# Reversing TensorE's three jobs of a step in the maximum rounds of a four-stage graph network

## The reference

```
for l in range(3):
    xi, xj = x[dst], x[src]
    m = concatenate([xi, xj - xi], axis=-1)
    h = relu(m @ W1[l] + b1[l])
    h = h @ W2[l] + b2[l]
    x = relu(segment_max(h, dst))
x = layernorm(x_before + x)
```

## Time and profile before

| | |
|---|---|
| two executions, median | 8951.76 us (8947.82 to 8955.71) |
| span of the profiled execution, first to last instruction | 8953.9 us |
| the profiled execution's own time | within the two above as far as its span tells; the page gives the span alone |
| TensorE matmul busy | 6143.5 us, 69% of the span |
| TensorE weight load busy | 3185.8 us, 36% |
| GpSimd busy | 5682.7 us, 63% |
| VectorE busy | 4170.1 us, 47% |
| ScalarE busy | 2476.2 us, 28% |
| TensorE on the chain that ended last | 41% of the span |

### The profile page before, as it was taken

The page is one execution under the profiler, slowest core; times in us unless marked ns, Lnnn a source line. Parts: engine busy times, 40 slices in busy tenths (PEclk is TensorE's granted clock), DMA queues, the critical chain, the costliest instruction groups (busy, mean ns, idle before and its releaser), DMA issues.

```text
span 8953.9 us, 145246 instructions
## 1 busy us (share of the span) xinstructions
PE 6143.5 (69%) x26339; PEld 3185.8 (36%) x26339; DVE 4170.1 (47%) x5692; ACT 2476.2 (28%) x6097; POOL 5682.7 (63%) x5873
## 2 busy tenths in 40 slices
PE   1333336666656666666333359999899999899997
PEld 0111124444434444443222224444344444344443
DVE  4444449999958999971333322222222222222222
ACT  0111114444434444431111112222222222222222
POOL 4777756666636666642777756666566666566665
PEclk9999996666656666655555555555555555555555
DMA  4666646666636565642333334444444444444443
GB/s 105 171 169 169 171 114 132 130 131 130 130 84 132 130 130 129 130 98 75 66 66 66 66 72 103 102 102 102 90 99 102 103 102 102 87 103 103 102 103 85
DMA packets 1847481, 981.41 MB, mean 110 GB/s; under 512 B 1290750, under 2 KB 1685374, under 8 KB 1847422
## 3 DMA queue, kind: packets, MB, share of 16 engines
q1 hardware_dynamic: 1660030, 786.84, 35.9%
q0 software_dynamic: 187392, 193.93, 13.3%
HBM read 714.25 MB, written 265.65 MB: 109 GB/s over the span
## 4 chain that ended last, share of the span: by engine, by line
PE 41%; issue 6%; POOL 6%; DVE 1%; ACT 1%; DMA 0%; SPq 0%; POOLq 0%; DVEq 0%
PE ps L847 13%; PE ps L824 12%; PE ps L820 10%; POOL rows L707 5%; PE ps L854 4%; PE ps L452 1%; PE ps L503 1%; PE ps L445 0%; POOL agg L717 0%; DMA rows<-src_table,idx 0%; DMA agg<-states_sum,last_i 0%; DVE split_r L326 0%; ACT split L317 0%; DVE split L328 0%; DMA states_sum<-hb 0%
## 5 line engine op out<-in xcount | busy, mean ns | idle before, releaser
L707 POOL DMA_INDIRECT rows<-src_table,idx x5656 | 5480.8, 969 | 2954.7 <-issue 1541.6
L820 PE MATMUL ps<-ident,rows 128*64 128x128 f32 x5656 | 1807.6, 405 | 1527.1 <-issue 738.9
L925 DVE TENSOR_TENSOR_SCAN st<-pen,st,ps 64x512 f32<-64x512 f32 x603 | 766.9, 1272 | 2696.9 <-PE ps L847 2692.1
L820 PEld LDWEIGHTS ps<-ident,rows 128*64 128x64 f32 x5656 | 773.1, 145 | 2038.4 <-issue 1766.2
L854 PEld LDWEIGHTS ps<-ident,st 64*128 64x128 f32 (+1 forms) x5656 | 797.7, 212 | 1584.9 <-issue 1555.0
L824 PE MATMUL ps<-sel,win 128*64 128x128 fp8e4 x7272 | 1281.9, 314 | 0.0
L847 PE MATMUL ps<-xe,w 64*64 64x512 f32 x1212 | 1190.1, 1083 | 0.0
L833 PE MATMUL ps<-sel,win 128*97 128x128 fp8e4 x4848 | 516.0, 282 | 837.4 <-issue 821.3
L754 ACT ACTIVATE pen<-sel 64x512 f32<-64x512 fp8e4 (+1 forms) x1010 | 628.1, 622 | 1468.3 <-DVE decay L989 1468.3
L854 PE MATMUL ps<-ident,st 64*128 64x64 f32 (+1 forms) x5656 | 1010.4, 330 | 23.5 <-DVE st L925 23.5
L759 ACT ACTIVATE hb<-ps 128x256 f32<-128x256 f32 (+1 forms) x1414 | 578.9, 409 | 1519.5 <-PE ps L854 819.4
(11 more groups left out here) (133 smaller groups left out, 3352.5 us busy)
## 6 DMA issues: line engine op xcount, KB each, us to landing
states_sum<-hb SPq DMA_DIRECT2D x1010, 128.0 KB
sel<-onehots SPq DMA_DIRECT2D x1010, 128.0 KB
win<-dst_table SPq DMA_DIRECT2D x1616, 72.8 KB
win<-dst_table SPq DMA_DIRECT2D x2424, 48.0 KB
rows<-src_table,idx POOLq DMA_INDIRECT x5656, 2.5
states_att<-hb SPq DMA_DIRECT2D x404, 194.0 KB
dst_b<-in_dst_row SPq DMA_DIRECT2D x202, 256.0 KB, 3.7
prev_b<-in_dst_prev SPq DMA_DIRECT2D x202, 256.0 KB, 4.4
```

Of the source, the lines that this page charges most:

```text
L707: pool.indirect_dma_start(rows[:, s, j, :], None, srcs[q.r], bass.IndirectOffsetOnAxis(ap=idx[:, s, j:j + 1], axis=0))\
L820: last = nc.tensor.matmul(o, rows[:, s, j, :], ident[:, :], is_transpose=True, start=True, stop=k != MAX)
L925: nc.vector.tensor_tensor_scan(st[0:kw, s % V, :], d0, d1, init, op0, op1).then_inc(q.st_ready.sem, 1)
```

## The change

In the MAX rounds the order of TensorE's list is reversed. The lags stay: in step t TensorE now transposes chunk t-2 back, lifts chunk t-1, and then turns chunk t. Nothing else differs; the instructions, their operands, waits and semaphores are the same, and so are all other engines' streams.

```
                 if k == ATT:
                     chunks(pe, (0, turn), (0, query), (1, score), (3, back))
                 elif k == MAX:
-                    chunks(pe, (0, turn), (1, lift), (2, back))
+                    chunks(pe, (2, back), (1, lift), (0, turn))
                 else:
                     chunks(pe, (0, turn), (1, back))
                 node_pe(pe, q)
```

## The result

The changed kernel took 9125.08 us (two executions, 9124.70 and 9125.46) against 8951.76 us: 173 us more, a ratio of 1.0194 with a 95% interval of 1.0175 to 1.0214. It is slower clear of the noise. The ratio itself is just inside 2%, but the interval has that line inside it.

A forecast was written before the change was run, and what follows sets the result against it. TensorE's full queue was taken to bound the MAX rounds; 3 rounds x (198 steps x 0.31 us + 0.9) = 187 us more, giving 9139 us, 2.1% slower; its own range 9109 to 9210, for 8 in 10 9098 to 9215.

The forecast's parts named there:

- TensorE's queue bounds the MAX rounds: MAX rounds: TensorE busy 1000 us of 1000, a step of 5.76 us, so each microsecond it stands still lengthens the program.
- The lift's stall: Lift behind its relu: starts 0.15 after turning, takes 0.68, plus latency, less back's 0.62; 0.31 us a step, 0.26 to 0.43.
- x: Latency from the relu's end until TensorE starts the lift: estimated 0.10 us, between 0.05 (node phase) and 0.22 (REL loop).
- The side of the 2% line: Relu exposed, 9109 to 9210 us, chance 0.81: 0.50 above the 2% line at 9131 us, 0.31 below.
- The weight load: Lift's weights: by the skill's rule the load could slip under back, up to 0.14 off each step, sum 104 us; given little.
- Back, penalty and scan at no cost: MAX step: scan over 1.62 us into the 3.25 of turning, 1.6 us of cover left; penalty doesn't hold up the scan.
- The ends of a round: First chunks of a MAX round 2.5 us longer, the end after the last turning 1.6 shorter: net 0.9 us a round.
- The sign to look for: Trace after: idle before the lift (L847), put down to ScalarE's xe (L777), about 0.3 us in some 600 steps.
- Rival C: TensorE's instruction stream refilled after each stall, or ScalarE late to the relu: 0.53 us a step, 9270 us; chance 0.07.
- Rival B: Back or an early load covers more of the relu: stall below 0.2 us, 8955 to 9056 us; chance 0.07.
- Rival D: Clock rises in the MAX rounds, at the joint of lift and turning: up to 460 us less, 8490 us; chance 0.05.
- The earlier copy is worth nothing: ScalarE's copy of chunk t-2 at about 1.45 us, not 2.67, lets SyncE's store and fetch leave sooner; gain worth nothing.

The follow-up runs named there:

- one step less: SyncE's store of a chunk three steps after its fetch, not four, in the MAX rounds: kernel before 9445.26 us, changed kernel 9130.70 us.
- both edits: Changed kernel's order of jobs plus the turning in two banks with transposes and products grouped by kind: 8667.5 us, 0.9682 of the kernel before.
- grouping alone: Kernel before, old order of jobs, with the turning's transposes and products grouped by kind over two banks: 8536.39 us, 0.9530 of the kernel before.

## Why the prediction was right, and what in it was off

*TensorE's queue bounds the MAX rounds.* Right. Shortening the turning by 0.69 us a step took 420 us off, and the idle that the new order adds, 0.29 a step, came back in full as time.

*The lift's stall is 0.15 + 0.68 + x - 0.62.* Right in each term: without back's cover the idle is 0.62 larger, with a relu of 0.47 the step is 5.84, with one 0.37 later it is 0.36 longer. Mis-sized in it was x alone. I took 0.10 between 0.05 and 0.22; it is 0.07, near the written-out code and far from the REL loop. The stall is 0.29 and not 0.31, 12 us in the sum.

*The side of the 2% line.* I had 0.50 of my 0.81 above it and said that it lay at x = 0.09. x came out below, so 1.94% and not 2.1%: the case was right, the heavier part of it was not.

*The weight load.* The lift's load starts at 6008.46, 0.07 behind the relu and not beside back at 6007.55: no load went ahead of its wait here. The rule of the Trainium skill, TensorE: Matmul & The Clock Gate, section Step-by-step: what each phase is for, that a load can be pulled ahead, did not show, and the measurement decides.

*Back, penalty and scan at no cost.* Right: with the lift moved alone the time is the same, 9126.73 us, and back would have cost 1.69 a step only if it had caught up with its own lift.

*The ends of a round.* I said 0.9 us a round; it is 0.6. With x these make the 13 us between the sum of 187 and the 174 above.

*The sign to look for.* I expected the idle row to name ScalarE's `xe`. It does so only in the written-out steps; for the loop the timeline was needed.

*Rival C, a refill after each stall.* Wrong: turning starts 1.89 us behind the lift's load (6008.46 to 6010.35) as before, with no second delay. *Rival B, the relu hides*, is wrong too: it wanted a stall below 0.2, and it is 0.29.

*Rival D, the clock.* It did not rise in the changed kernel. In the grouped one with the new order it did, to 0.99, so a rise was not out of reach; whether the joint of lift and turning that I named brought it is not shown, and there it was worth only some 36 us. The changed kernel stayed at 1.2 GHz with TensorE 96% busy. With that its trace too disagrees with the Trainium skill, TensorE: Matmul & The Clock Gate, Part 1, by which sustained matmul work releases the full clock.

*The earlier copy is worth nothing.* Right on the chips on which the kernel was timed, and the weakest sentence of the prediction: it holds only while fetches are early, by a margin that one step less used up.

## What to carry to other kernels

In a queue that never waits, the age of each job's input is what pays for latency: here reversing the list of lagged jobs took one step of age from the lift and from back. What then shows is the length of the producer less the job that still lies between, here 0.90 less 0.62 us. Ask of each pair what its producer takes, and order the jobs so that each has a cover at least as long: back, with a whole turning for its 1.69 us, cost nothing. The same reversal also frees buffers sooner, and where fetches were late it won by 3.3%; so name the bound before the order. And before turning jobs round, look inside one for changes between kinds of instruction: five fewer of them a chunk gave 4.7%.

## What the runs showed of the hardware

- TensorE pays about 0.135 us at a change between a transpose and a product here: taking five of seven out of a turning shortened it from 3.25 to 2.56 us. It pays as much from a product to the lift and from back to the turning (0.24 against 0.11), so transpose against product is not the whole rule.
- After a wait in a loop, TensorE's load follows the end of ScalarE's relu by 0.07 us, where the REL round's turning took 0.22 behind VectorE's product.
- One chip ran the same program in 10424 us against 8952 to 8956 on the others. In the traces of the changed orders there the matmuls' records, whose ends are modelled, are as long as elsewhere (1.93 us for the lift's pair), but in the long steps the relu that follows a turning starts mostly 0.6 to 3 us later.
- With the same instructions, the granted clock left 0.50 in the MAX rounds in one order of jobs (both edits, seven times) and never in the other (grouping alone).
